# Denominators of eight chunks summed into one PSUM bank, inverted once, read back from DRAM

## What is computed

```python
qkv = concat(q, k, v)                       # 1x1 projections, 3 x 512 channels
pw = conv1x1(depthwise5x5(qkv))             # a second set of 3 x 512 channels
f = concat(qkv, pw).reshape(B, -1, 3 * d, N)      # d = 8, N = 4096
query, key_, value = relu(f[:, :, :d]), relu(f[:, :, d:2*d]), f[:, :, 2*d:]
value_pad = concat(value, ones)
scores = einsum('bhdn,bhen->bhde', value_pad, key_)
out = einsum('bhde,bhen->bhdn', scores, query)
out = out[:, :, :-1] / (out[:, :, -1:] + 1e-15)
y = batchnorm(conv1x1(out)) + x
```

## Time and profile before

| | us |
|---|---|
| median of 3 runs | 5286.34 (5278.08 to 5292.49) |
| the profiled execution | 5281.64 |
| its span, first to last instruction | 5279.8 |
| TensorE busy | 4916.6 (93%) |
| VectorE busy | 3335.9 (63%) |
| ScalarE busy | 2155.2 (41%) |
| GpSimd busy | 1238.7 (23%) |
| mean granted clock of TensorE | 0.964 of full speed |

### The profile page before, as it was taken

The page is one execution under the profiler, slowest core; times in us unless marked ns, Lnnn a source line. Parts: engine busy times, 40 slices in busy tenths (PEclk is TensorE's granted clock), DMA queues, the critical chain, the costliest instruction groups (busy, mean ns, idle before and its releaser), DMA issues. The chain is left out here.

```text
span 5279.8 us, 65622 instructions
## 1 busy us (share of the span) xinstructions
PE 4916.6 (93%) x22760; PEld 3466.3 (66%) x22760; DVE 3335.9 (63%) x3794; ACT 2155.2 (41%) x3927; POOL 1238.7 (23%) x1030
## 2 busy tenths in 40 slices
PE   8999999999999999999999996899999989998958
PEld 7887887887887887887887883344444434443423
DVE  3656656656656656656666554687588578847865
ACT  3333333333333333333333330355555455545555
POOL 2332342342341442432332330000200020011002
PEclk9999999999999999999999997999999999999969
DMA  6545545545545555555555544343334243424313
GB/s 198 173 164 184 178 160 186 177 161 182 177 167 179 172 175 177 175 173 177 176 174 178 173 153 147 128 144 134 124 128 157 97 148 129 159 100 142 116 41 113
DMA packets 349341, 817.69 MB, mean 155 GB/s; under 512 B 28752, under 2 KB 61904, under 8 KB 346768
## 3 DMA queue, kind: packets, MB, share of 16 engines
q1 hardware_dynamic: 349072, 813.72, 45.5%
HBM read 521.69 MB, written 291.93 MB: 154 GB/s over the span
## 5 line engine op out<-in xcount | busy, mean ns | idle before, releaser
L705 POOL TENSOR_TENSOR toeplitz<-taps 128x512 f32<-128x512 f32 x768 | 899.6, 1200 | 1070.4 <-PE bank L403 1070.4
L403 PEld LDWEIGHTS bank<-toeplitz,columns 128*128 128x128 f32 x8192 | 961.1, 193 | 15.2
L403 PE MATMUL bank<-toeplitz,columns 128*128 128x128 f32 x8192 | 960.8, 276 | 0.0
L1001 PE MATMUL bank<-att,w_proj 128*128 128x512 f32 x2048 | 908.7, 598 | 34.9 <-DVE centred L1286 23.8
L602 DVE RECIPROCAL den_sb<-den_sb 128x512 f32<-128x512 f32 x256 | 856.1, 3344 | 29.3 <-ACT den_sb L477 27.1
L1001 PEld LDWEIGHTS bank<-att,w_proj 128*128 128x128 f32 x2048 | 392.6, 192 | 532.0 <-issue 523.4
L319 PE MATMUL bank<-x_hi,w_hi 128*128 128x512 f32 x1536 | 609.7, 397 | 18.9 <-DVE x_lo L577 18.8
L1334 POOL TENSOR_TENSOR centred<-centred,x_out 128x512 f32<-128x512 f32 x128 | 164.7, 1321 | 1941.9 <-ACT centred L1148 1941.9
L321 PE MATMUL bank<-x_lo,w_hi 128*128 128x512 f32 x1536 | 600.0, 391 | 0.0
L320 PE MATMUL bank<-x_hi,w_lo 128*128 128x512 f32 x1536 | 599.4, 390 | 0.0
L643 DVE TENSOR_SCALAR ckey_t<-bank 128x256 f32<-128x256 f32 x256 | 107.5, 420 | 775.7 <-PE bank L403 775.7
(11 more groups left out here) (113 smaller groups left out, 6048.3 us busy)
## 6 DMA issues: line engine op xcount, KB each, us to landing
x_sb<-in_x_tiled SPq DMA_DIRECT2D x128, 1024.0 KB, 6.3
tiles_dram<-tiles SPq DMA_DIRECT2D x128, 867.0 KB, 6.1
loaded<-tiles_dram SPq DMA_DIRECT2D x256, 433.5 KB, 3.5
att_dram<-out_sb SPq DMA_DIRECT2D x256, 256.0 KB, 3.9
att<-att_dram SPq DMA_DIRECT2D x64, 1024.0 KB, 6.1
xb<-x_dram SPq DMA_DIRECT2D x128, 330.0 KB, 3.2
x_out<-in_x_pad SPq DMA_DIRECT2D x32, 1056.0 KB, 5.3
x_dram<-x_out SPq DMA_DIRECT2D x32, 1056.0 KB, 8.4
```

Source lines behind the costliest of these rows:

```text
L403: last = nc.tensor.matmul(bank[:, v * M:(v + 1) * M], columns[:, h % 2, t - T_K, v + b, a * HT:(a + TO) * HT], w[:, t, d, :], start=(d == ...
L705: last = nc.gpsimd.tensor_tensor(toeplitz[:, h % 2, t, :].rearrange("p (d o r) -> p d o r", o=HD, r=PL), tap, point, ALU.mult)
L1001: last = nc.tensor.matmul(P_BANKS[m][:, :], w_proj[:, i * HALF + k, m * P:(m + 1) * P], att[:, i, k, :], start=(i == 0 and k == 0), stop=( ...
```

## The change

The key sums of a half are laid out as eight 128 x 128 blocks side by side, all zero but for 16 columns each: block j holds its 16 head columns at 16 j. The eight matmuls of the eight chunks accumulate in the one bank, so that row 16 j + h holds head h, chunk j, and nothing is repeated on partitions. VectorE then adds 1e-15 and takes one reciprocal of 128 x 512 for the whole half. The inverse goes to DRAM (256 KB), and comes back a chunk at a time, each of its 16 rows read to 8 partitions (256 KB again), into a tile of two buffers. `divide` multiplies by that tile. ScalarE's part (`denominators`) is gone. `w_out` is gone too: the mixed weights are written over `w_proj`, so the next load of it waits until they are in DRAM. The mask is 128 x 16.

The eight matmuls of half 0 run at the end of the plain part, behind the last score; those of half 1 behind projection 1 of the next plain part. The divides of half 0 follow heads 4 to 11, those of half 1 two by two in chunks 4 to 7, ahead of `split_x`.

```diff
+                def write_inverse(it, half):
+                    sp.wait_ge(inverted, 2 * it + half + 1)
+                    sp.dma_start(dram["inverse"][half], den_sb[:, :]).then_inc(den_written, 16)
+
+                def load_inverse(it, half, j):
+                    sp.wait_ge(divided, START + at(it, half, j) - 1)
+                    sp.dma_start(inverse[:, j % 2, :],
+                                 dram["inverse"][half][j * SH:(j + 1) * SH, None, :].to_broadcast([SH, HD, CH])
+                                 ).then_inc(inverse_loaded[j % 2], 16)
...
                 def plain(it, conv_of):                       # SyncE
...
                         write_tiles(it, j)
                         if conv_of is not None:
+                            if j == 2:
+                                write_inverse(conv_of, 1)
+                            if j == 3:
+                                sp.wait_ge(den_written, 16 * START + 32 * conv_of + 32)
+                                for i in range(2):
+                                    load_inverse(conv_of, 1, i)
                             if j == 4:
                                 write_w(conv_of, 1)
+                            if j == 6:
                                 load_w_proj(it, 0)
-                            if j >= 2:
-                                spill(conv_of, 1, j - 2)
+                            if 4 <= j < NCH - 1:
+                                for i in range(2 * j - 8, 2 * j - 6):
+                                    spill(conv_of, 1, i)
+                                    load_inverse(conv_of, 1, i + 2)
...
                 def conv(it, last):                           # SyncE
...
+                        if h == 1:
+                            write_inverse(it, 0)
+                        if h == 2:
+                            sp.wait_ge(den_written, 16 * START + 32 * it + 16)
+                            for i in range(2):
+                                load_inverse(it, 0, i)
+                        if 5 <= h < NCH + 5:
+                            spill(it, 0, h - 5)
+                            if h - 3 < NCH:
+                                load_inverse(it, 0, h - 3)
...
-                def denominate(it, half, j):
-                    pe.wait_ge(scores_masked, 2 * it + half + 1)
+                def denominate(it, half):
+                    pe.wait_ge(sums_placed, 2 * it + half + 1)
...
-                    pe.wait_ge(den_evac, START + at(it, half, j))
-                    nc.tensor.matmul(DEN_BANK[:, :], score_d[:, half, :], rows((relu_q, relu_c)[half], j),
-                                     start=True, stop=True).then_inc(summed, 1)
+                    pe.wait_ge(den_evac, START + 2 * it + half)
+                    for j in range(NCH):
+                        last = nc.tensor.matmul(DEN_BANK[:, :], score_d[:, j * P:(j + 1) * P], rows((relu_q, relu_c)[half], j),
+                                                start=(j == 0), stop=(j == NCH - 1))
+                    last.then_inc(summed, 1)
...
                 def plain(it, conv_of):                       # TensorE
...
-                            if j >= 1:
-                                denominate(conv_of, 1, j - 1)
+                            if j == 1:
+                                denominate(conv_of, 1)
...
-                    if conv_of is not None:
-                        denominate(conv_of, 1, NCH - 1)
                     score(it, NCH - 2)
                     turn(it, NCH - 1)
                     score(it, NCH - 1)
+                    denominate(it, 0)
...
                 def conv(it):                                 # TensorE
...
-                        if h % 2:
-                            denominate(it, 0, h // 2)
...
                 def final(it):                                # TensorE
                     conv(it)
+                    denominate(it, 1)
                     turn_scores(it, 1)
-                    denominate(it, 1, 0)
                     mix_weights(it, 1)
-                    for j in range(1, NCH):
-                        denominate(it, 1, j)
...
                 def mask_scores(it, half):                    # VectorE
...
+                    apart, last = P + SH, (NCH - 1) * (P + SH)
+                    nc.vector.tensor_scalar(score_d[:, 0:last].rearrange("p (j s) -> p j s", s=apart)[:, :, 0:SH],
+                                            mask[:, None, :].to_broadcast([P, NCH - 1, SH]), key_sum[:, 0:1], None, ALU.mult)
+                    nc.vector.tensor_scalar(score_d[:, last:last + SH], mask[:, :], key_sum[:, 0:1], None,
+                                            ALU.mult).then_inc(sums_placed, 1)
...
+                def invert(it, half):
+                    dve.wait_ge(summed, 2 * it + half + 1)
+                    dve.wait_ge(den_written, 16 * START + 16 * (2 * it + half))
+                    nc.vector.tensor_scalar(den_sb[:, :], DEN_BANK[:, :], EPS_ATT, None, ALU.add).then_inc(den_evac, 1)
+                    dve.wait_ge(den_evac, START + 2 * it + half + 1)
+                    nc.vector.reciprocal(den_sb[:, :], den_sb[:, :]).then_inc(inverted, 1)
+
                 def divide(it, half, j):
-                    dve.wait_ge(den_evac, START + at(it, half, j) + 1)
-                    nc.vector.reciprocal(den_sb[:, :], den_sb[:, :]).then_inc(inverted, 1)
-                    dve.wait_ge(inverted, at(it, half, j) + 1)
+                    dve.wait_ge(inverse_loaded[j % 2], 16 * (NCH * it + NCH // 2 * half + j // 2) + 16)
...
                 def plain(it, conv_of):                       # VectorE
...
                             keys_by_position(it, j - 2)
-                            if conv_of is not None:
-                                divide(conv_of, 1, j - 2)
+                        if conv_of is not None:
+                            if j == 2:
+                                invert(conv_of, 1)
+                            if j >= 4:
+                                for i in range(2 * j - 8, 2 * j - 6):
+                                    divide(conv_of, 1, i)
                         if j + 1 < NCH:
                             split_x(it, j + 1)
                         value(it, j)
...
                     mask_scores(it, 0)
+                    invert(it, 0)
...
                 def final(it):                                # VectorE
                     conv(it, False)
-                    divide(it, 1, 0)
+                    invert(it, 1)
                     mixed_weights(it, 1)
-                    for j in range(1, NCH):
+                    for j in range(NCH):
                         divide(it, 1, j)
```

More of the change, by code:

```diff
@@ L131, in attention @@
         w_out_written = sem("w_out_written")
+        sums_placed = sem("key_sums_placed")
         summed = sem("den_summed")
+        den_written = sem("inverse_written")
+        inverse_loaded = [sem(f"inverse_loaded{i}") for i in range(2)]
         den_evac = sem("den_evac")
@@ L198, in load_w_proj @@
                 def load_w_proj(it, half):
+                    if not (isinstance(it, int) and it == 0 and half == 0):
+                        sp.wait_ge(w_out_written, 16 * START + 16 * (2 * it + half))
                     sp.dma_start(w_proj[:, :], io["projT"][it % HS + HS * half]).then_inc(w_proj_loaded, 16)
@@ L264, in conv @@
                             write_w(it, 0)
+                        if h == 8:
                             load_w_proj(it, 1)
-                        if h >= 3 and h % 2:
-                            spill(it, 0, h // 2 - 1)
+                        if h == 1:
[8 more added lines that the diff above has]
+                                load_inverse(it, 0, h - 3)
                     for i in range(2):
@@ L300, in final @@
                     conv(it, True)
+                    write_inverse(it, 1)
                     write_w(it, 1)
+                    sp.wait_ge(den_written, 16 * START + 32 * it + 32)
+                    for i in range(2):
+                        load_inverse(it, 1, i)
                     for j in range(NCH):
                         spill(it, 1, j)
+                        if j + 2 < NCH:
+                            load_inverse(it, 1, j + 2)
                     for s in out_written:
@@ L343, in turn_scores @@
                     pe.wait_ge(scores_masked, 2 * it + half + 1)
-                    nc.tensor.matmul(W_BANKS[half][:, 0:P], score_n[:, half, :], ident[:, :],
+                    nc.tensor.matmul(W_BANKS[half][:, 0:P], score_n[:, :], ident[:, :],
                                      start=True, stop=True, is_transpose=True).then_inc(score_turned, 1)
@@ L472, in value_by_position @@
                     copy(value_t[:, j % 2, :, 0:P], VALUE_BANK[:, :].rearrange("p (n m) -> p n m", m=P)).then_inc(value_t_ready, 1)
-                def denominators(it, half, j):
-                    act.wait_ge(summed, at(it, half, j) + 1)
-                    act.wait_ge(divided, START + at(it, half, j))
```

(22 more changed lines are left out.)

36 lines of the change are left out of this document (16 added, 20 removed).

## The result

| | before | after |
|---|---|---|
| median of 20 runs each, us | 5282.93 (5275.81 to 5292.49) | 5293.29 (5284.54 to 5307.15) |
| span of the profiled execution, us | 5279.8 | 5288.7 |
| mean granted clock of TensorE | 0.964 | 0.975 |

The ratio is 1.0022, with a 95% interval of 1.0016 to 1.0028: about 12 us slower, within the 0.3% that the prediction called no change. I had forecast 43 us faster. The time lies inside the range, which it owes to the range's width of 131 us.

What follows compares the result with a forecast made beforehand. It took TensorE, busy 193.2 of a pass's 201.1 us, as the bound, not VectorE. Terms 101 + 3 - 11 - 60 + 10 gave 43 us faster, 5243 by the median; forecast 5205 to 5275, range 5185 to 5316.

Steps and rivals of the forecast that it cites:

- rival 4: Work nobody waited for is moved; seam gain and new wait cancel within 16 us: 5286 us, chance 0.15.
- A: Seam from plain part to convolution: denominator matmuls cover the branch; gain 7.2 us a seam, 101 us, plus 3 at the exit.
- B: End of the convolution: without a denominator step TensorE stands about 0.7 us before the score matmuls, 11 us lost.
- C: Plain part, chunks 4 to 6: split_x waits behind divides for inverses; 4.0 us a part, 60 us lost.
- D: Drained end of the attention stage, half 1 of the last pass: gain 8 to 12 us, taken as 10.
- Clock kept: At the seam after the change: with new idle of 2.9 us, TensorE's granted clock was to stay up.
- rival 2: Inverses' loads rule chunks 4 to 7: 7 us a plain part instead of 4, and low clock; 5314 us, chance 0.17.
- E: Other edits, such as fewer reciprocals, no den_sb copies, the invert in chunk 2 and more DMA traffic: counted at nothing.
- Rival 1: Inverses come in time in the plain part, under 4 us each: 5183 us, chance 0.11.
- Rival 3: The branch at the seam isn't hidden, so 81 us aren't gained: 5324 us, chance 0.09.
- a pass is not between 196 and 200 us: Sign for the pass time: outside these bounds the prediction was to count as wrong.

Runs made afterwards that it cites:

- Experiment 7: Changed kernel with split_x ahead of the divides in chunks 4 to 7, divides of chunks 6 and 7 behind the masked sums: 5196.12 us, 0.9836 of before.
- experiment 1: Changed kernel with VectorE's split_x put ahead of the two divides in chunks 4 to 7: 0.9957 of before.
- experiment 6: Changed kernel with the seam's denominator run of half 0 doubled, 32 matmuls instead of 16: 1.0198 of before.
- 9: Kernel before with value_t and key_t of chunk 7 ahead of the last den_sb copy and divides, loads of heads 2 and 3 held back: 0.9915 of before.
- 8: Changed kernel, split_x ahead of the divides, last two divides behind the masked sums, loads of heads 2 and 3 held until head 0's q: 0.984 of before.
- 5: Changed kernel with SyncE's loads of heads 2 and 3 issued behind write_q of head 0, not ahead of the branch: 0.9969 of before.
- 3: Changed kernel with the eight denominator matmuls of half 0 moved from the seam to behind head 0, none over the branch: 1.0152 of before.
- 4: Kernel before with value_t of chunk 7 copied before the last den_sb copy and key_t of chunk 7 made before the last two divides: 0.9976 of before.
- experiment 2: Changed kernel with the first two inverse loads of half 1 issued ahead of load_x in SyncE's chunk 3: 1.0023 of before.

## Why the prediction was wrong

What came true is rival 4, to which I gave 0.15: gain and new wait cancel within 16 us. The waits that the forecast named are all there, but its price for the branch was not; its sum is a small difference of large terms, and every term missed to the same side.

| us over the stage | predicted | measured |
|---|---|---|
| A, seams and the exit | +104 | 15 x 5.2 = +77 |
| B, end of the convolution | -11 | 16 x 1.1 = -18 |
| C, new wait in the plain part | -60 | 15 x 4.9 = -73 |
| D, drained end | +10 | +8 |
| the program's start | 0 | -2 |
| sum | +43 | -8 |

The stage's last divide ends 7.5 us later than before (3228.36, now 3235.82), which is that sum. The program's start is the first turn of a chunk, at 36.49 instead of 34.85; why is open.

**A. This is the step that failed.** "0.3 + 4.2, and some 0.6 of register work behind it, at most 6.5 us, is less than 6.9" took the branch's 4.2 as a property of the branch. I had read its median and its largest value and not asked what stood in the DMA queue at that moment. Before, the four head loads were issued from 1683.69 on, 5.7 us ahead of the branch at 1689.4, with one spill behind them, on SyncE's timeline:

```profile
1683.69 1.75 SPq L210 DMA_DIRECT2D loaded<-tiles_dram  x4
1688.05 0.34 SPq L221 DMA_DIRECT2D att_dram<-out_sb  x1
```

Now they are issued from 1696.77 on, 3.3 us ahead of it, with two spills behind them. Both ends moved: TensorE is 0.7 us earlier (8.7 us behind the start of score 5, 9.4 before), and the loads are later, since they wait for the last `tiles`, whose copy (line 614, at 1692.44) stands behind two divides that waited for their inverses. So C's wait feeds A's branch, a link between two terms that I had summed as if they stood apart. Experiment 7 bears it out: the loads go out 4.6 us behind the start of score 5 with those two divides moved, 5.7 in the changed kernel, 7.2 in experiment 1, which leaves them in place. 20.2/14 = 1.44 us a pass came back as "issue". The rest of A: key_t cost 1.54 and 0.78 (1.45 and 0.79 predicted), score_d 0.98 instead of 0.65, probably because two writes of `score_d` now stand ahead of TensorE where the earlier trace rows had one (not tested); and head 0 is 5.7 instead of 5.4, since behind two of the idles the clock fell after all (7.2 us there, 5.5 in the others). "Clock kept" was nearly right: the granted clock over the stage (110 to 3190 us) is 1.00, after 0.98 before. That the queue takes the run was right, and by experiment 6 for the right reason: 33 were queued, 34 had been read from the earlier trace rows.

The Trainium skill (TensorE: Matmul & The Clock Gate, Architectural detail) gives that queue a depth of 64; experiment 6, with 64 instructions in the run, shows 33 as the profile counts them (every float32 matmul twice), and the measurement decides.

**B.** 1.1 us a pass instead of 0.7. The wait itself was right, on TensorE's timeline before the score matmuls (0.68 at 1797.81, 10.8/16 = 0.68 in the list of waits). Of the other 0.4 I can name 0.2 at most, a wait for `toeplitz` of 2.8 us over the stage.

**C.** The waits were right in place and sum: 76.0 less the first 12.6 is 63.4 us in 42 waits, 57 more than before, where I had said some 60 and three a pass. The single stalls were not: ahead of projections 5, 6 and 7 they are 1.4, 2.2 and 0.4 us on average over the 15 passes, where I had 1.9, 1.3 and 0.8, so that the sum of 4.0 is in part luck. In the pass shown, divide 0 begins 9.4 us after projection 3's end at 1646.0 (9.75 predicted). What I left at nothing was the clock: behind the 2.2 us of the pass shown stands a projection that took 1.6 us more. I had put that into rival 2, as something that comes only with longer idles. Five such stretches in plain parts make 8 us; some 7 more I can't name. The divides of two chunks took 3.23 us at 1666.65, while GpSimd was at work (1665.11 to 1668.46), and 2.04 at 1655.44, when it was not, which the upper bound held and the value taken did not.

**D.** From the masks (3201.8) to the last divide 34.0 us, 42.5 before, within the 30.5 to 34.5 given. The one pair of inverse buffers makes it go in steps on VectorE's timeline:

```profile
3223.29 1.07 DVE L638 TENSOR_TENSOR out_sb<-relu_c,inverse 128x256 f32<-128x256 f32 x2 [2.72 <-DMA inverse<-inverse_dram]
3225.38 1.07 DVE L638 TENSOR_TENSOR out_sb<-relu_c,inverse 128x256 f32<-128x256 f32 x2 [1.02 <-DMA inverse<-inverse_dram]
3228.32 1.07 DVE L638 TENSOR_TENSOR out_sb<-relu_c,inverse 128x256 f32<-128x256 f32 x2 [1.88 <-DMA inverse<-inverse_dram]
```

**E.** Held, save for the program's start.

**The rivals.** Rival 1 (inverses in time) is out by 402.3 us of VectorE's waits for them. The Trainium skill (DMA: Bandwidth & Descriptors, Anatomy of one DMA) states its 2.0 us plus bytes at 436 GB/s for transfers that GpSimd issues; SyncE issues these. Rival 2's threshold of 6.9 us a plain part was not reached. Rival 3 had the right place, and I dismissed it by rows that showed the branch in another neighbourhood. My bounds for "a pass is not between 196 and 200 us" did not bite: a pass of 199.9 lies inside them, because I took the stretch of 201.1 us in the earlier trace rows for a pass, whose mean was 199.1.

## What to carry to other kernels

When a change shortens the way to a point, ask what is under way there at the new time; a duration read at the old time is not a constant. Where a wait for a transfer enters an engine's order, put the work that the critical engine needs ahead of it at every place, not only at the first one that shows. And when a forecast is the difference of two terms of 60 to 100 us, give "they cancel" the chance that the terms' errors have.

## What the runs showed of the hardware

**A taken branch of TensorE costs what its instruction fetch has to wait for.** Medians, with what is issued to the DMA queue around it and how far into the branch the first instruction packet starts:

| kernel | data issued around the branch | branch, us | packet, us |
|---|---|---|---|
| experiment 6 | four loads, landed | 3.4 | 1.0 |
| 9 | two loads of four, no spill near | 3.7 | 1.0 |
| 8 | two loads 4 us ahead, spills behind its start | 4.0 | 0.9 |
| before | four loads 5.6 us ahead, one spill | 4.2 | 1.5 |
| 7 | four loads 4.1 us ahead, spills behind its start | 4.9 | 2.1 |
| 5 | two loads and two spills ahead | 5.2 | 2.8 |
| 3 | four loads about its start, spills behind | 5.3 | 2.9 |
| 4 | four loads 2.7 us ahead | 5.8 | 3.4 |
| 1 | four loads 4.6 us ahead, two spills | 6.6 | 3.6 |
| 2 | four loads and two spills ahead, as after | 7.1 | 4.6 |
| after | four loads 3.0 us ahead, two spills | 7.2 | 4.5 |

Work queued on TensorE does not lengthen it (6) and hides it (3).

The Trainium skill (DMA: Bandwidth & Descriptors, Queues, rings and completion order) says that a DMA engine takes turns between the queues that have work, packet by packet. By that alone a fetch would hardly notice the data. The runs show it start 4.5 us into the branch behind them and 1.0 us without; whether it waits in the DMA engines or ahead of them, no run here shows.

**The queue of TensorE** held 33 instructions when the sequencer came to the branch in experiment 6, of the 64 in the run, as the profile counts them.

**Two reads of 256 KB that spread rows to 8 partitions, put ahead of an x load,** delay it by 3 us (9.2 instead of 6.0, experiment 2).
